# A vision block with attention scan and sixteen experts: low parts of three weight pieces moved from TensorE to VectorE, one row array per group, engine lists written anew

## The chip, the cores and the metric

The kernel runs on one core of one Trainium2 chip. The metric is the device time in microseconds (us) of one execution, where less is better. Each time below is one run, and the median of three is what counts. The profiled execution is a run of its own, with its own time.

## The reference

32 images of 96x96 are cut into 36 patches of 256 pixels each, projected to 192 channels, and a class token is put ahead, so each image has 37 rows. A block with a two-sided exponential scan over the rows (attention without a softmax matrix) and a gated square-ReLU layer is added, and then a mixture of 16 experts, of which each row takes 4 out of the 2 best of 4 groups, with 2 shared experts.

```python
h = concatenate([cls_tok, patches(x) @ W.T], axis=1)          # 32 x 37 x 192
# h = h + attention block(layernorm(h)):
x = layernorm(h); k, v, r = x @ Wk.T, x @ Wv.T, x @ Wr.T
y = bi_wkv(decay / T, first / T, k, v)                        # scans from both sides
x = x + sigmoid(r) * y @ Wo.T
g = ln(x); x = x + sigmoid(g @ Wr_f.T) * (square(relu(g @ Wk_f.T)) @ Wv_f.T)
# h = h + expert layer(layernorm(h)):
c = routing weights of 16 experts (sigmoid scores, top 2 of 4 groups, top 4, normalized, x 2.5)
hid = silu(x @ gWg + gbg) * (x @ gWu + gbu)                   # for each expert
out = sum(c * (hid @ gWd + gbd)) + shared experts
```

All is float32. A product with float32 accuracy is made of products of a rounded high part and the remaining low part of both factors.

## The kernel before, in words

The 1184 rows (32 images of 37) are worked on in four groups of 6, 10, 10 and 6 images: 222, 370, 370 and 222 rows. For each group there are these tracks of work, and the order lists name their steps as TRACK+GROUP:step.

- F, the front: patches to rows (tok0, tok1), normalization (stats1 to ln1), transposes and split into high and low part (tr1), products k, kt, v, rt, r, the two scans on VectorE (scan0, scan1, ab00 to ab11), exponentials on ScalarE (exps, weights), the quotient (recip, z), the output product (o0, o1) and the sum (x10, x1s, x1). Z:x0 on ScalarE makes the normalized rows that the sum starts from.
- M, the middle: normalization 2 (stats2 to ln2, tr2), the gate (rf), six pairs of an up product and a down product (up0 to up5, mix0 to mix5) with ReLU and square on ScalarE between them, the gated sum (gated, h1), normalization 3 (stats3 to ln3, tr3) and the routing (logits to routed).
- G, Y, S, X, D: the experts. 14 units (2 shared, 12 of 128 expert channels): TensorE makes a gate product (g0 to g13) and a value product (v1 to v13) into two PSUM banks, ScalarE applies SiLU (Y:e0 to e13), VectorE multiplies (S:s0 to s13) and applies the routing weights (X:x2 to x13), and TensorE adds up the outputs (D:d0 to d13). D:cT and C:cT transpose the routing weights and copy them; SyncE writes them to memory and spreads them over the partitions into the array gates.
- W, the weights: pieces of weights are loaded into a ring of four raw buffers. ScalarE copies each into its rounded high part (hi). The low part (lo) is raw - hi. For most pieces VectorE subtracts. For the six pieces of the experts, egu0 to egu5 (128 partitions, 1024 columns), the track L does it: TensorE multiplies raw by the identity and hi by the negative identity into PSUM array PA (L1162, L1163), and ScalarE copies PA into lo (L394). PA is also what the D steps add up into.

No engine chooses its next step at run time. PE_ORDER, ACT_ORDER, DVE_ORDER and POOL_ORDER are lists written out in the file; advance() runs the generator of each track up to the named step. Within a list each engine works strictly in order, and semaphores make it wait for what other engines owe it: a step that is not ready holds up all that stand behind it. SyncE's transfers stand in the order of the code. The ring buffer of a piece comes free when its low part is done.

Steps that need a neighbour: the experts of group g start at G:g0, once M:tr3 has split the normalized rows (stack3). ScalarE copies the rows of F:tok into the array h0, two of which serve four groups in turn; base holds the residual sum and h1 the rows after the middle, also two each. ScalarE's functions stand in tables: when the next activation needs another table than the last, an ACT_TABLE_LOAD stands ahead of it.

## Time and profile before

| | us |
|---|---|
| runs | 268.15, 268.33, 270.0 |
| median | 268.33 |
| profiled execution | 268.65 |
| its span | 266.8 |
| TensorE (PE) busy | 233.7 (88%) |
| VectorE (DVE) busy | 195.0 (73%) |
| ScalarE (ACT) busy | 147.6 (55%) |
| GpSimd (POOL) busy | 18.0 (7%) |

The span is the time from the first to the last instruction in the trace; the execution's own time lies 1.85 us above it. PE is TensorE's matmuls and PEld its weight loads, which overlap them; matmul ends are modelled, so neighbouring matmuls seem to overlap a little. The granted clock of TensorE is given as a share of 2.4 GHz. Times "from" and "at" are from the start of the span. A line number is that of the kernel before.

### The profile page before, as it was taken

Reading aid. Unit: us, or ns where it says so; the run is one execution under the profiler, and the core shown is the slowest. Engines: PE = TensorE matmul, PEld = TensorE weight load, DVE = VectorE, ACT = ScalarE, POOL = GpSimd, SP = SyncE. Lnnn points to the kernel's source line nnn. Section 1 sums busy time; section 2 is a strip of 40 time slices with the busy share of each in tenths; the row PEclk is TensorE's granted clock in tenths of the full one; section 3 lists DMA queues with packets and bytes.
Section 4 is the critical chain, followed back from the end, with each engine's and each line's share of the span. In section 5 each row is a group of like instructions: output and inputs, shape, how many; then the busy total and the mean of one; then the engine's idle time right before and its main releaser. Section 6 shows DMA issues by size and latency. Waiting matters only on the chain.

```text
span 266.8 us, 4316 instructions
## 1 busy us (share of the span) xinstructions
PE 233.7 (88%) x1436; PEld 211.5 (79%) x1436; DVE 195.0 (73%) x496; ACT 147.6 (55%) x305; POOL 18.0 (7%) x24
## 2 busy tenths in 40 slices
PE   0484968588878999999999999999999999999994
PEld 0373428465557899998999999999999999899993
DVE  4459898999997999989986599877731445654442
ACT  2489886989449997462756894144444332122220
POOL 4100402030011000030010000101000010000000
PEclk9998699999999999999999999999999999999999
DMA  5679550000000280000002430000014510014311
GB/s 150 210 254 337 176 184 2 0 0 0 0 2 1 47 195 2 2 0 0 4 26 68 174 105 4 0 1 0 2 30 160 164 37 2 1 35 106 68 34 37
DMA packets 12823, 17.49 MB, mean 66 GB/s; under 512 B 2144, under 2 KB 10882, under 8 KB 12674
## 3 DMA queue, kind: packets, MB, share of 16 engines
q1 hardware_dynamic: 11272, 16.20, 20.7%
q10 hardware_dynamic: 1530, 1.02, 1.4%
q8 instruction: 12, 0.20, 0.3%
q14 instruction: 9, 0.07, 0.1%
HBM read 16.22 MB, written 0.99 MB: 65 GB/s over the span
## 4 chain that ended last, share of the span: by engine, by line
PE 65%; DVE 16%; ACT 9%; issue 5%; DMA 2%; POOL 1%; SPq 0%; DVEq 0%; POOLq 0%; ACTq 0%
PE PG L958 17%; PE PA L978 15%; PE PG L960 11%; PE PF L978 4%; PE PA L1162 3%; DVE S L721 3%; PE PQ L958 2%; PE PX L995 2%; PE PF L995 2%; DVE K L745 2%; DMA w_tok<-in_w_tok 2%; PE PF L985 1%; DVE S L726 1%; DVE hid L901 1%; POOL rstd L374 1%
## 5 line engine op out<-in xcount | busy, mean ns | idle before, releaser
L553 ACT ACTIVATE act<-PG,columns 128x222 f32<-128x222 f32 (+3 forms) x56 | 28.4, 506 | 63.7 <-PE PG L960 60.0
L958 PE MATMUL PG<-stack,hi_egu 128*128 128x222 f32 (+1 forms) x288 | 62.1, 324 | 0.8 <-DVE hid L901 0.5
L901 DVE SCALAR_TENSOR_TENSOR hid<-PG,columns,act 128x222 f32<-128x222 f32 (+1 forms) x52 | 27.1, 520 | 30.9 <-PE PG L960 15.7
L958 PEld LDWEIGHTS PG<-stack,hi_egu 128*128 128x128 f32 x288 | 45.2, 190 | 4.9 <-DVE hid L901 2.9
L978 PE MATMUL PA<-w_ed,hid 128*124 128x192 f32 (+1 forms) x240 | 46.0, 327 | 0.7 <-DVE hid L914 0.7
L960 PE MATMUL PG<-stack,lo_egu 128*128 128x222 f32 (+1 forms) x192 | 42.7, 304 | 0.0
L978 PEld LDWEIGHTS PA<-w_ed,hid 128*124 128x124 f32 (+1 forms) x240 | 38.6, 183 | 1.1 <-issue 1.0
L960 PEld LDWEIGHTS PG<-stack,lo_egu 128*128 128x128 f32 x192 | 31.7, 190 | 0.0
L374 POOL TENSOR_TENSOR rstd<-var,minus_half 112x2 f32<-112x2 f32 (+3 forms) x12 | 15.2, 1266 | 198.7 <-DVE var L647 198.7
L914 DVE TENSOR_TENSOR hid<-hid,gates 128x222 f32<-128x222 f32 (+1 forms) x48 | 21.7, 463 | 8.2 <-DMA gates<-c_rows 7.4
L978 PE MATMUL PF<-w_down,mix_hid 128*124 128x192 f32 (+1 forms) x120 | 23.2, 327 | 0.2 <-ACT mix_hid L525 0.2
L978 PEld LDWEIGHTS PF<-w_down,mix_hid 128*124 128x124 f32 (+1 forms) x120 | 19.2, 183 | 0.5 <-ACT mix_hid L525 0.5
L1162 PE MATMUL PA<-gates,columns 128*128 128x512 f32 x24 | 14.4, 686 | 5.4 <-ACT hi_egu L383 3.3
L958 PE MATMUL PQ<-stack,hi_up 128*128 128x222 f32 (+1 forms) x72 | 15.9, 329 | 1.0 <-ACT relu L519 1.0
L519 ACT ACTIVATE relu<-PQ 128x222 f32<-128x222 f32 (+1 forms) x24 | 10.0, 415 | 12.1 <-PE PQ L960 12.1
L721 DVE TENSOR_TENSOR_SCAN S<-E,S 128x333 f32<-128x333 f32 (+1 forms) x16 | 16.3, 1066 | 0.0
L402 ACT ACTIVATE norm<-h,shift,rstd 124x192 f32<-124x192 f32 (+1 forms) x20 | 9.6, 537 | 7.1 <-DVE shift L653 7.1
L958 PEld LDWEIGHTS PQ<-stack,hi_up 128*128 128x128 f32 x72 | 11.3, 190 | 2.6 <-issue 2.6
L745 DVE RECIPROCAL K<-K 128x222 f32<-128x222 f32 (+3 forms) x8 | 11.9, 1520 | 0.1
L1162 PEld LDWEIGHTS PA<-gates,columns 128*128 128x128 f32 x24 | 4.6, 211 | 8.6 <-issue 8.3
L525 ACT ACTIVATE mix_hid<-relu 128x222 f32<-128x222 f32 (+1 forms) x24 | 10.8, 452 | 0.8
L667 DVE TENSOR_TENSOR stack<-full,stack 128x222 fp32r<-128x222 f32 (+3 forms) x16 | 7.4, 461 | 5.1 <-ACT full L413 4.9
(230 smaller groups left out, 418.6 us busy)
## 6 DMA issues: line engine op xcount, KB each, us to landing
gates<-in_w_egu SPq DMA_DIRECT2D x6, 512.0 KB, 4.0
gates<-c_rows SPq DMA_DIRECT2D x16, 138.8 KB, 2.8
gates<-c_rows SPq DMA_DIRECT2D x16, 92.5 KB, 2.7
w_ed<-in_w_ed SPq DMA_DIRECT2D x1, 1152.0 KB, 8.0
gates<-c_rows SPq DMA_DIRECT2D x12, 83.2 KB, 2.8
gates<-in_w_up SPq DMA_DIRECT2D x2, 384.0 KB, 3.7
pat<-in_patches SPq DMA_DIRECT2D x2, 370.0 KB, 4.2
gates<-c_rows SPq DMA_DIRECT2D x16, 46.2 KB, 2.6
```

The costliest lines, as they stand in the source:

```text
L374: nc.gpsimd.tensor_tensor(small[n]["rstd"][0:G.tp, 0:cols, 0:G.tiles], small[n]["var"][0:G.tp, 0:cols, 0:G.tiles], minus_half[0:G.tp, 0:co ...
L525: nc.scalar.activation(mix_hid[:, m % 2, 0:G.n], relu[:, 0:G.n], ACT.Square).then_inc(act_square, 1)
L553: nc.scalar.activation(act[128 - gate:128, n % 2, 0:G.n], PG[0:gate, gate_bank(n), 0:G.n], ACT.Silu, bias=bias).then_inc(act_silu, 1)
L721: step(V_.tensor_tensor_scan(run(x, d), run(E1[:, d * WK:d * WK + wk], d), run(x, d), 0.0, ALU.mult, ALU.add))
L745: step(V_.reciprocal(K[:, s], K[:, s]))
L901: V_.scalar_tensor_tensor(out, PG[part, 1, 0:G.n], bias, act[part, i, 0:G.n], ALU.add, ALU.mult).then_inc(mul_done, 1)
L914: V_.tensor_tensor(out, out, gates[:, n - SCH, 0:G.n], ALU.mult).then_inc(hid_ready, 1)
L958: mm(out, w_hi[:, slot, cols], x[:, p, 0:G.n], start=(p == 0), stop=False, skip_group_check=True)
L960: last = mm(out, w_lo[:, p, cols], x[:, p, 0:G.n], start=False, stop=(p == 1), skip_group_check=True)
L978: last = mm(tile_out(P, G, t), src[:, G.ts[t]:G.ts[t] + G.tp], w, start=start and t != 1, stop=stop, skip_group_check=True)
L995: last = mm(out, src[:, G.ts[t]:G.ts[t] + G.tp], w, start=(i == 0 and t == a), stop=(i == len(parts) - 1), skip_group_check=True)
L1162: mm(PA[:, k, 0:512], ident32, raw[n % RING][:, 512 * k:512 * k + 512], start=True, stop=False, skip_group_check=True)
```

## The change

It does five things.

1. The low parts of egu0, egu1 and egu2 stay with TensorE and ScalarE; those of egu3, egu4 and egu5 are made by VectorE with one subtraction each, as for the other pieces.
2. Each group has an array of its own for its rows (stream), which holds in turn what h0, base and h1 held. The waits that guarded the reuse of those arrays go away. Some other arrays are shared: norm2 is x1, norm3 is gate_r, Zm is the front of V, and ReLU writes into mix_hid, where the square is taken in place. The waits that these need are added or moved.
3. The array gates gets HELD = 4 periods of 3 chunks, of which there are 4, by way of gate_slot.
4. SyncE fetches group 3's patches ahead of group 0's gate rows.
5. The lists of TensorE, ScalarE and VectorE are written anew. POOL_ORDER stays.

```diff
 PERIODS = ECH // 3
+HELD = 4
-LOW_ON_PE = [p[0] for p in PIECES if p[0].startswith("egu")]
+LOW_ON_PE = [p[0] for p in PIECES if p[0] in ("egu0", "egu1", "egu2")]
+LOW_ON_DVE = [p[0] for p in PIECES if p[0] not in LOW_ON_PE]
...
-        gates = sb("gates", [128, ECH, N])
-        flat_gates = gates[:, :, :].rearrange("p c n -> p (c n)")
-        raw = [flat_gates[:, i * RING_COLS:(i + 1) * RING_COLS] for i in range(RING)]
+        gates_raw = sb("gates", [128, max(3 * HELD * N, RING * RING_COLS)])
+        gates = gates_raw[:, 0:3 * HELD * N].rearrange("p (c n) -> p c n", n=N)
+        raw = [gates_raw[:, i * RING_COLS:(i + 1) * RING_COLS] for i in range(RING)]
+
+        def gate_slot(g, chunk):
+            return (g * ECH + chunk) % (3 * HELD)
...
-        h0 = [sb(f"h0_{i}", [TP, TILES, C]) for i in range(2)]
+        stream = [sb(f"h_{g}", [G.tp, G.tiles, C]) for g, G in enumerate(GROUP)]
         x1, gate_r = (sb(n, [TP, TILES, C]) for n in ("x1", "gate_r"))
-        base, h1 = ([sb(f"{n}_{i}", [TP, TILES, C]) for i in range(2)] for n in ("base", "h1"))
-
-        norm = [None, *(sb(f"norm{i}", [TP, TILES, C]) for i in (1, 2, 3))]
+
+        norm = [None, sb("norm1", [TP, TILES, C]), x1, gate_r]
         full = [None, *(sb(f"full{i}", [128, 2, N]) for i in (1, 2))]
...
-        Zm = sb("Zm", [128, N])
+        Zm = V[:, 0:N]
...
-        relu, mix_hid = sb("relu", [128, N]), sb("mix_hid", [128, 2, N])
+        mix_hid = sb("mix_hid", [128, 2, N])
...
                 if g == 0:
                     sp.wait_ge(lo_done, len(PIECES) - len(LOW_ON_PE))
                     sp.wait_ge(pe_low, len(LOW_ON_PE))
-                    for first, periods, done in ((0, 1, gates_in[0]), (1, PERIODS - 1, gates_in[1])):
+                    for first, periods, done in ((0, 1, gates_in[0]), (1, HELD - 1, gates_in[1])):
...
-                    return
                 for j in range(PERIODS):
-                    if g:
-                        sp.wait_ge(hid_ready, at(hid_ready, g - 1, 3 * (j + 1)))
+                    q = g * PERIODS + j - HELD
+                    if q < 0:
+                        continue
+                    sp.wait_ge(hid_ready, at(hid_ready, q // PERIODS, 3 * (q % PERIODS + 1)))
...
-                        sp.dma_start(gates[a:b, 3 * j + chunk, 0:n],
+                        sp.dma_start(gates[a:b, gate_slot(g, 3 * j + chunk), 0:n],
...
             for n in range(13, len(PIECES)):
                 piece(n)
             patches(2)
+            patches(3)
             gates_across(0)
-            patches(3)
             for g in range(1, len(GROUP)):
                 gates_across(g)
             for g in range(len(GROUP)):
...
             G, P = GROUP[g], front_banks(g)
             for bank, a, b in G.banks:
                 act_e.wait_ge(pe_tok, at(pe_tok, g, bank + 1))
-                if g >= 2 and bank == 0:
-                    act_e.wait_ge(x1_ready, at(x1_ready, g - 2, 1))
-                nc.scalar.activation(h0[g % 2][0:G.tp, a:b, :], rows_of(P[bank], G, a, b), ACT.Copy).then_inc(tok_out, 3 - G.rounds)
+                nc.scalar.activation(stream[g][0:G.tp, a:b, :], rows_of(P[bank], G, a, b), ACT.Copy).then_inc(tok_out, 3 - G.rounds)
                 yield f"tok{bank}"
             act_e.wait_ge(rstd_ready[1], at(rstd_ready[1], g, 1))
...
             act_e.wait_ge(pe_kvr, at(pe_kvr, g, 2))
             tails(K, lower, lower)
             yield "kt"
+            since(act_e, pe_o, g)
             tails(V, upper, upper)
             yield "vt"
             act_e.wait_ge(act_kvr, at(act_kvr, g, 2))
...
         def act_first_rows(act_e, g):
             G = GROUP[g]
-            since(act_e, norm_ready[2], g)
+            since(act_e, pe_transposed[2], g)
...
                     since(act_e, act_square, g)
                 else:
                     act_e.wait_ge(act_square, at(act_square, g, m))
-                nc.scalar.activation(relu[:, 0:G.n], PQ[:, 0:G.n], ACT.Relu).then_inc(act_relu, 1)
-                act_e.wait_ge(act_relu, at(act_relu, g, m + 1))
                 if m >= 2:
                     act_e.wait_ge(pe_mix, at(pe_mix, g, m - 1))
                 elif m == 0:
                     since(act_e, pe_mix, g)
-                nc.scalar.activation(mix_hid[:, m % 2, 0:G.n], relu[:, 0:G.n], ACT.Square).then_inc(act_square, 1)
+                nc.scalar.activation(mix_hid[:, m % 2, 0:G.n], PQ[:, 0:G.n], ACT.Relu).then_inc(act_relu, 1)
+                act_e.wait_ge(act_relu, at(act_relu, g, m + 1))
+                nc.scalar.activation(mix_hid[:, m % 2, 0:G.n], mix_hid[:, m % 2, 0:G.n], ACT.Square).then_inc(act_square, 1)
                 yield f"mix{m}"
             act_e.wait_ge(rstd_ready[3], at(rstd_ready[3], g, 1))
-            act_norm_rows(act_e, g, 3, h1[g % 2])
+            act_norm_rows(act_e, g, 3, stream[g])
...
             yield "x1s"
             v.wait_ge(x1_out, at(x1_out, g, 2))
             rs = (slice(0, G.tp), slice(0, G.tiles))
-            V_.tensor_tensor(base[g % 2][rs], h0[g % 2][rs], x1[rs], ALU.add).then_inc(x1_ready, 1)
+            V_.tensor_tensor(stream[g][rs], stream[g][rs], x1[rs], ALU.add).then_inc(x1_ready, 1)
             yield "x1"
         def edge_e1(wk):
...
             v.wait_ge(act_rf, at(act_rf, g, 1))
             v.wait_ge(pe_mix, at(pe_mix, g, UPS))
-            if g >= 2:
-                v.wait_ge(out_stored[g - 2], 16 * GROUP[g - 2].tiles)
-            h = h1[g % 2]
+            x = stream[g]
             for bank, a, b in G.banks:
                 step(V_.scalar_tensor_tensor(gate_r[0:tp, a:b, :], gate_r[0:tp, a:b, :], 1.0, rows(PF, G, bank, a, b), ALU.add, ALU.mult))
             yield "gated"
             settle()
-            step(V_.scalar_tensor_tensor(h[rs], gate_r[rs], 0.5, base[g % 2][rs], ALU.mult, ALU.add))
+            step(V_.scalar_tensor_tensor(x[rs], gate_r[rs], 0.5, x[rs], ALU.mult, ALU.add))
             yield "h1"
             settle()
...
 PE_ORDER = _order(
-    "F0:tok0 F0:tr1a F0:tr1b F1:tok0 F0:k F0:kt F1:tok1 F0:v F0:rt F0:r L:egu0 F1:tr1a F1:tr1b L:egu1 L:egu2 F0:o0 F1:k",
+    "F0:tok0 F0:tr1a F0:tr1b F1:tok0 F0:k F1:tok1 F0:kt F0:v F0:rt F0:r L:egu0 F1:tr1a F1:tr1b L:egu1 F0:o0 F1:k F1:kt F1:v",
...
-    "M0:mix2 M0:up4 M0:mix3 M0:up5 M0:mix4 M0:mix5 F2:tr1b L:egu5 F1:o0 F1:o1 M0:tr3 F2:k M0:logits G0:g0 F2:kt G0:g1 G0:v1",
-    "F2:v G0:g2 F2:rt D0:cT G0:v2 G0:g3 D0:d1 D0:d0 M1:tr2 G0:v3 F2:r G0:g4 G0:v4 G0:g5 M1:rf M1:up0 D0:d2 D0:d3 G0:v5 D0:d4",
-    "G0:g6 G0:v6 F3:tok0 D0:d5 G0:g7 G0:v7 D0:d6 G0:g8 M1:up1 G0:v8 M1:mix0 M1:up2 G0:g9 D0:d7 M1:mix1 M1:up3 G0:v9 G0:g10",
+    "M1:tr2 F2:r G0:v2 G0:g3 F3:tok0 G0:v3 G0:g4 D0:cT D0:d1 D0:d0 M1:rf M1:up0 G0:v4 G0:g5 M1:up1 M1:mix0 M1:up2 M1:mix1",
...
 ACT_ORDER = _order(
-    "F2:exps F2:weights Y0:e6 F3:tok0 Y0:e7 M1:rf M1:mix0 Y0:e8 M1:mix1 Y0:e9 M1:mix2 M1:mix3 M1:mix4 Y0:e10 F3:ln1 M1:mix5",
+    "M0:logits Y0:e0 Y0:e1 F2:kf F2:v M1:ln2 Y0:e2 F2:rt M1:tr2 Y0:e3 F2:r F2:exps C0:cT Z2:x0 Y0:e4 M1:rf M1:mix0 Y0:e5",
+    "F3:tok0 M1:mix1 M1:mix2 F2:weights M1:mix3 Y0:e6 F3:ln1 Y0:e7 M1:mix4 Y0:e8 F3:tr1a F3:tr1b M1:mix5 Y0:e9 Y0:e10 Y0:e11",
...
 DVE_ORDER = _order(
+    "W:egu3 F0:x1s F0:x1 M0:stats2 M0:mean2 F1:scan0 M0:var2 F1:scan1 M0:ln2 F1:e1 F1:sb0 W:egu4 F1:sb F1:top0 F2:stats1",
+    "M0:var3 F2:tr1 F1:x1s M0:ln3 F1:x1 W:egu5 M0:tr3 M1:stats2 M0:biased M1:mean2 M0:logits M1:var2 F2:scan0 S0:s0",
...
```

The lists move steps in many places. Three of them follow, as the built programs have them; instructions of a kind that follow each other stand in one row with their count.

VectorE, from the statistics of group 0's third normalization (M0:mean3) to the subtractions of M0:tr3 (stack_0), before:

```order
L647 TENSOR_SCALAR var<-mv 112x2
L759 TENSOR_TENSOR x<-x,PX 124x384
L653 SCALAR_TENSOR_TENSOR shift<-mv,rstd 112x2
L667 TENSOR_TENSOR stack<-full,stack 128x370
L667 TENSOR_TENSOR stack<-full,stack 64x370
L759 TENSOR_TENSOR x<-x,PX 124x192
L765 TENSOR_TENSOR base<-h_1,x 124x576
L667 TENSOR_TENSOR stack_0<-PF,stack_0 128x222
L667 TENSOR_TENSOR stack_0<-PF,stack_0 64x222
```

The same place now:

```order
L763 TENSOR_TENSOR x<-x,PX 124x384
L651 TENSOR_SCALAR var<-mv 112x2
L671 TENSOR_TENSOR stack<-full,stack 128x370
L671 TENSOR_TENSOR stack<-full,stack 64x370
L763 TENSOR_TENSOR x<-x,PX 124x192
L657 SCALAR_TENSOR_TENSOR shift<-mv,rstd 112x2
L769 TENSOR_TENSOR h<-h,x 124x576
L602 TENSOR_TENSOR lo_egu<-gates,hi_egu 128x1024
L671 TENSOR_TENSOR stack_0<-PF,stack_0 128x222
L671 TENSOR_TENSOR stack_0<-PF,stack_0 64x222
```

The low part of egu5 stands directly ahead of M0:tr3, and the shift of ln3 has moved behind F2:tr1 and F1:x1s.

TensorE, from group 0's last down products of the middle (L978, M0:mix) to the transposes of M0:tr3 (PF from norm), before:

```order
L958 MATMUL PQ<-stack,hi_up 128x222 x3
L960 MATMUL PQ<-stack,lo_up 128x222 x2
L978 MATMUL PF<-w_down,mix_hid 112x192 x4
L985 MATMUL PX<-columns,norm 128x124 x3
L1162 MATMUL PA<-gates,columns 128x512
L1163 MATMUL PA<-hi_egu,minus_ident 128x512
L1162 MATMUL PA<-gates,columns 128x512
L1163 MATMUL PA<-hi_egu,minus_ident 128x512
L995 MATMUL PX<-w_o,Zm 124x192 x2
L995 MATMUL PX<-w_o,Zt 124x192 x2
L995 MATMUL PX<-w_o,Zm 124x192
L995 MATMUL PX<-w_o,Zt 124x192
```

The same place now, up to M0:tr3 and F2:kt:

```order
L960 MATMUL PQ<-stack,hi_up 128x222 x3
L962 MATMUL PQ<-stack,lo_up 128x222 x2
L980 MATMUL PF<-w_down,mix_hid 112x192 x4
L997 MATMUL PX<-w_o,V 124x192 x2
L997 MATMUL PX<-w_o,Zt 124x192 x2
L997 MATMUL PX<-w_o,V 124x192
L997 MATMUL PX<-w_o,Zt 124x192
L960 MATMUL PX<-stack,hi_k 128x370 x3
L962 MATMUL PX<-stack,lo_k 128x370 x2
L987 MATMUL PF<-columns,gate_r 128x112 x4
L960 MATMUL PX<-stack,hi_k 128x370 x3
L962 MATMUL PX<-stack,lo_k 128x370 x2
```

Nothing stands between the last down products and the o products of group 1 (PX from w_o) any more, and both k products of group 2 stand ahead of the router's products.

ScalarE, around the exponentials of group 2 (E, S and mx in place; R is the last), before:

```order
L553 ACTIVATE act<-PG,columns 128x222
L472 ACT_TABLE_LOAD
L472 ACTIVATE E<-E,columns 128x2x370
L472 ACTIVATE E<-E,columns 128x2x185
L473 ACTIVATE S<-S 128x2x555
L477 ACTIVATE mx<-mx 128x555 x2
L480 ACTIVATE mx<-mx 128x555
L481 ACTIVATE R<-R 128x555
L553 ACT_TABLE_LOAD
L553 ACTIVATE act<-PG,columns 128x222
```

Now the first half of it:

```order
L476 ACT_TABLE_LOAD
L476 ACTIVATE E<-E,columns 128x2x370
L476 ACTIVATE E<-E,columns 128x2x185
L477 ACTIVATE S<-S 128x2x555
L568 ACTIVATE hid_s<-PQ 17x222
L493 ACTIVATE x<-h,shift,rstd 124x192 x3
L557 ACT_TABLE_LOAD
L557 ACTIVATE act<-PG,columns 128x222
```

And, eleven rows later, the second:

```order
L481 ACT_TABLE_LOAD
L481 ACTIVATE mx<-mx 128x555 x2
L484 ACTIVATE mx<-mx 128x555
L485 ACTIVATE R<-R 128x555
L527 ACTIVATE mix_hid<-PQ 128x370
L529 ACTIVATE mix_hid<-mix_hid 128x370
L557 ACT_TABLE_LOAD
L557 ACTIVATE act<-PG,columns 128x222
```

The program before has six table loads, the changed one eight.

## Rows read from the trace of the kernel before

**Rows 1.** The page: busy us per engine, and busy tenths in 40 slices.

```profile
PE 233.7 (88%) x1436; PEld 211.5 (79%) x1436; DVE 195.0 (73%) x496; ACT 147.6 (55%) x305; POOL 18.0 (7%) x24
...
PE   0484968588878999999999999999999999999994
...
DVE  4459898999997999989986599877731445654442
```

**Rows 2.** Busy time in four stretches: us of each engine, clock, DMA.

```profile
20.00:80.00 60.00, 44.00 (x210) 30.72 (x209) 56.20 (x108) 46.23 (x94) 7.39 (x4) 0.94 0.23 78
80.00:104.00 24.00, 22.31 (x153) 20.28 (x153) 21.36 (x63) 21.71 (x41) 0.85 (x1) 1.00 0.31 68
104.00:224.00 120.00, 119.47 (x773) 115.75 (x773) 87.53 (x239) 60.46 (x132) 5.95 (x6) 1.00 0.14 43
224.00:267.00 43.00, 38.56 (x270) 36.77 (x268) 20.52 (x64) 8.88 (x19) 0.00 (x0) 1.00 0.19 44
```

**Rows 3.** VectorE in order of time: start, us, instruction, idle before.

```profile
29.72 0.17 DVE L653 SCALAR_TENSOR_TENSOR shift<-mv,rstd 124x6 f32<-124x6 f32 x1 [1.22 <-POOL rstd L374]
...
55.45 1.32 DVE L715 TENSOR_TENSOR S<-S,V 128x1110 f32<-128x1110 f32 x1
...
78.41 0.80 DVE L667 TENSOR_TENSOR stack<-PF,stack 128x222 fp32r<-128x222 f32 x2
```

**Rows 4.** TensorE in order of time.

```profile
26.97 2.05 PE L1162 MATMUL PA<-gates,columns 128*128 128x512 f32 x2 [3.32 <-ACT hi_egu L383]
...
69.14 0.90 PE L978 MATMUL PF<-w_down,mix_hid 128*112 128x192 f32 x4 [0.21 <-ACT mix_hid L525]
...
70.20 1.03 PE L1162 MATMUL PA<-gates,columns 128*128 128x512 f32 x2
...
73.68 0.89 PE L995 MATMUL PX<-w_o,Zm 128*124 128x192 f32 x4 [1.13 <-issue]
...
75.93 0.59 PE L995 MATMUL PX<-w_o,Zm 128*124 128x192 f32 x2 [0.71 <-DVE x L759]
...
80.51 0.68 PE L958 MATMUL PX<-stack,hi_k 128*128 128x370 f32 x3
81.03 0.50 PE L960 MATMUL PX<-stack,lo_k 128*128 128x370 f32 x2
81.37 0.49 PE L958 MATMUL PG<-stack,hi_sgu 128*128 128x222 f32 x3
```

**Rows 5.** Line 598: operation, count, shortest/median/longest ns, starts.

```profile
L598 DVE TENSOR_TENSOR lo_r<-gates,hi_r x1: 685/685/685, 13.2 to 13.2; 128x512 fp32r<-128x512 f32 x1
...
L598 DVE TENSOR_TENSOR lo_sgu<-gates,hi_sgu x1: 951/951/951, 25.4 to 25.4; 128x768 fp32r<-128x768 f32 x1
```

**Rows 6.** VectorE's waits from 0 to 80: total us, times, longest.

```profile
DVE shift L653 <- POOL rstd L374: 2.7, 3, 1.2
...
DVE x L759 <- PE PF L995: 0.6, 1, 0.6
...
DVE stats L635 <- ACT x L489: 0.4, 1, 0.4
```

**Rows 7.** GpSimd in order of time.

```profile
26.99 2.69 POOL L374 TENSOR_TENSOR rstd<-var,minus_half 124x6 f32<-124x6 f32 x1 [14.22 <-DVE var L647]
```

**Rows 8.** ScalarE in order of time, ahead of 80 us.

```profile
52.92 1.41 ACT L472 ACTIVATE E<-E,columns 128x740 f32<-128x740 f32 x2
54.23 1.11 ACT L473 ACTIVATE S<-S 128x1110 f32<-128x1110 f32 x1
...
62.07 1.05 ACT L383 ACTIVATE hi_egu<-gates 128x1024 fp32r<-128x1024 f32 x1
```

**Rows 9.** ScalarE in order of time, behind 80 us.

```profile
94.93 1.28 ACT L472 ACT_TABLE_LOAD   x1
```

**Rows 10.** Busy time in two stretches; the clock is the number before the last two.

```profile
25.00:31.00 6.00, 4.03 (x6) 1.84 (x6) 4.78 (x13) 5.34 (x11) 2.69 (x1) 0.50 0.76 271
32.00:38.00 6.00, 4.43 (x15) 2.11 (x14) 5.83 (x9) 5.42 (x8) 0.00 (x0) 1.00 0.53 160
```

32 lines of the change are left out of this document (16 added, 16 removed), and 97 rows, old and new, of tables (ACT_ORDER, DVE_ORDER, PE_ORDER).

## The prediction

> **What bounds the kernel now.** I read the engines' busy times and the forty slices first, then the busy times of four stretches, then VectorE's waits, then the instructions in order of time around the places where the lists differ. By the shares TensorE is the busiest (233.7 us of 266.8), but its slices show two different kernels: in its first thirteen slices, until 87 us, the digits are mostly 4 to 8, and from there on all are 9 but the last; VectorE's row is the other way round, 8s and 9s with one 7 from 20 to 133 us, and 7s and less over the last third [rows 1]. In numbers: from 20 to 80 us VectorE is busy for 56.2 of 60 us and TensorE for 44.0; from 80 to 104 us TensorE has 22.3 of 24; from 104 to 224 us it has 119.5 of 120 [rows 2]. So there is a first part, which ends when group 0's rows are normalized for the experts (M0:tr3, the two subtractions at 78.41 us [rows 3]) and which VectorE sets, and a second part, which TensorE sets. A microsecond of TensorE is worth something only if it is removed behind that point; a microsecond of VectorE is worth something only ahead of it, or where TensorE waits for it.
>
> **The low parts.** Three pieces leave TensorE. The last of them began at 70.20 us and was over 1.13 us, the idle time that stands in the next row, before 73.68 us: some 2.3 us, so 6.9 us leave TensorE, and three copies from PSUM leave ScalarE. All three stood in the first part, and behind the last one TensorE sat idle because VectorE's z of group 1 was not there yet [rows 4]. Cover is what is removed here, not path: I cost the removal itself at 0. It becomes idle time of TensorE unless something else is pulled ahead.
>
> VectorE gets three subtractions over 1024 columns. The trace has none of that width; the nearest are 951 ns for 768 columns and 685 ns for 512 [rows 5], 266 ns per 256 columns, so 1.22 us, and 1.18 us from start to start since neighbours overlap a little: **+3.5 us** for three. All three stand ahead of M0:tr3, the last directly ahead of it (first order listing), and no other VectorE work crosses that point, so the whole 3.5 us fall into the part that VectorE sets.
>
> **What the new lists give back on VectorE.** Until 80 us VectorE's waits hold three that the lists fill: 1.2 us of the 2.7 us for GpSimd's root, the one before the shift at 29.72 us [rows 3, 6], 0.6 us for group 0's o product, and 0.4 us ahead of group 2's statistics [rows 6]. Group 1's variance now goes out ahead of F0:e1, some 4 us of VectorE work before the shift that needs it, where the root took 2.69 us [rows 7]; W:egu3 stands where the 0.6 us wait was, W:egu4 ahead of the 0.4 us one. **-2.2 us**.
>
> **What they cost on ScalarE.** Group 1's F1:sa started at 55.45 us [rows 3], right when ScalarE's exponentials (52.92 us, then 54.23 us for 1.11 us) ended: there both engines are tight. The copy hi_egu5, 1.05 us, stood at 62.07 us and now stands ahead of these exponentials [rows 8]. I leave 0.3 us of it to ScalarE's short idle times, so **+0.75 us**; the ends are 0 and 1.05 us.
>
> First part together: 3.5 - 2.2 + 0.75 = +2.0 us until the experts of group 0 can start.
>
> **Second part.** TensorE's own list for it is shorter by one step: F2:kt, at 80.51 us behind the start of G0, is now done ahead of it: 0.86 us from its start at 80.51 us to the next product at 81.37 us [rows 4]. **-0.85 us**. From 80 to 104 us TensorE was idle for 24 - 22.3 = 1.7 us [rows 2]. F3:tok0 can fill some of that: group 3's patches are now fetched before group 0's gate rows, and the product stands between G0:g3 and G0:v3 instead of behind G0:v6. F2:scan0 also stands in VectorE's wait for the first SiLU. I take **-1.0 us**; the ends are 0 and -1.7 us. Behind 104 us there is no idle to win [rows 2], and the lists of group 3's experts, which make the tail, are the same in both kernels.
>
> **ScalarE's table loads.** The third pair of listings shows what the names of the steps hide. F2:exps and F2:weights stood together between two SiLU; now SiLU steps stand between them, so the function table is changed twice more in this stretch. A change takes 1.28 us [rows 9], so 2.57 us more for an engine that has 21.7 of 24 us busy there [rows 2]. Who waits: behind the second new load stands e6, and G0:g7 waits for e6. Between G0:g5 and G0:g7 TensorE's new list puts M1:up1 to up4, mix0 to mix2 and three D0 steps: up1 to up4 alone make 3.4 us by the 0.86 us of F2:k, which has the same five products over 370 columns [rows 4], more than both loads. I take 0; the ends are 0 and +2.6 us.
>
> **Edits at no cost.** One array per group: the sum into stream takes the place of the sum into base, one VectorE instruction for another; the wait for the stores of group g-2 falls away at M2 and M3, where TensorE is full whatever VectorE does [rows 2]. The gate array holds four periods, as many as there are, so slots and waits of its transfers stay. ReLU and square still are two ScalarE instructions; the wait for mix(m-2), now ahead of ReLU, is met, since TensorE issues mix(m-2) ahead of up(m). Zm in V: F1:vt must wait for F0:o, which stands ahead of F1:k. x0 now waits for TensorE's transposes M0:tr2 instead of for the norm: that is in the 0.75 us.
>
> **Sum.** +2.0 - 0.85 - 1.0 + 0 = +0.15 us on a profiled execution of 268.65 us: 268.8 us. That execution lies 0.3 us above the median of the runs, 268.33 us, so **268.5 us**. What a measurement of this kernel can tell from no change is about 1%, 2.7 us: faster means below 265.65, slower above 271.0.
>
> **Rivals.** *TensorE's saving comes through* (25%). VectorE's 3.8 us of idle time between 20 and 80 us [rows 2] would take in 3.3 us of the added 3.5, the exponentials would not be late, and TensorE would fill all its 1.7 us: +3.5 - 3.3 - 0.85 - 1.7 = -2.35 us, and up to -3.5 us if VectorE's idle time from 80 to 104 us (24 - 21.4 us [rows 2]) closes by another 1.2 us: 265.9 to 264.8 us, 265.3 us in the middle. For it: TensorE is the busiest engine and loses 6.9 us [rows 1, 4]. Against it: none of the 6.9 us lay in the part that TensorE sets.
>
> *ScalarE's table loads uncover* (18%). One place: e4 to e6 of group 0. If M1's steps are not ready when the list wants them, TensorE stands before G0:g5 or G0:g7 for both loads. +2.6 us on the sum: 271.1 us, **slower**. It decides from the point where e6 comes later than TensorE has work between g5 and g7; every microsecond behind that is TensorE's. For it: with 21.7 of 24 us busy ScalarE has 2.3 us to spare [rows 2], less than 2.6 us. Against it: M1's steps are early in all lists.
>
> *TensorE's clock falls* (15%). In the trace TensorE idled for 3.32 us before 26.97 us [rows 4], and from 25 to 31 us its granted clock was 0.50, 1.2 instead of 2.4 GHz; from 32 to 38 us it was 1.00 [rows 10]. The mean from 20 to 80 us is 0.94 [rows 2], which the fall at 25 us makes up alone, so the gap of 1.13 us before 73.68 us [rows 4] brought none. With the piece at 70.20 us gone, TensorE has nothing between M0:mix5, which started at 69.14 us [rows 4], and F1:o0, which waits for z at about 73.7 us: a gap of some 4 us, longer than the one that went with the fall. At half clock F1:o0 (two products of 0.89 us), F1:o1 (two of 0.59 us) and F2:k (0.86 us) take 3.8 us more [rows 4], and all stand ahead of M0:tr3, which leads to the experts. About half of it lies beside VectorE's work of the same time, so +1.9 us on the sum, 270.4 us. The Trainium skill, page "TensorE: Matmul & The Clock Gate", section "Why this matters for your kernels", warns of just this: longer idle gaps between bursts of matmuls take the engine back to half rate. By that rule the lower clock comes for certain, and the sum would be 270.4 us; the trace agrees with it at 26.97 us, and has no such gap at this place.
>
> The forecast itself has 42%. That the change would not do what it says is excluded: the built program has three pieces on each engine.
>
> **From the cases.** Faster by over 1%: two thirds of the first rival (17%) and the lower end of the forecast (5%), 22%. Slower by over 1%: half of the second (9%), a third of the third (5%) and the upper end of the forecast (4%), 18%. Within 1%: 60%. The range goes from the first rival's middle less 0.4 us, 264.9 us, to just above the second rival's time, 271.2 us; the forecast's own is 266.8 to 270.2 us.
>
> **What would show it.** VectorE's M0:tr3 at 80.4 us instead of 78.4; its three new rows at 1.2 us each; no wait of over 0.5 us for the root before F1:ln1; F1:sa at 56.2 us; TensorE's stretch behind 104 us as full as before; eight table loads instead of six; and the granted clock between 70 and 80 us, 1.00 if I am right in my sum. I would be wrong in the sum if M0:tr3 stood at 79 us or earlier, and wrong in the mechanism if TensorE showed idle time behind 104 us.

## The result, and the profile after

In its first set of runs the changed kernel took 271.35 us in the median (268.79 to 273.04, 20 runs) against 268.5 us (267.84 to 270.7, 20 runs) for the kernel before in the same set: a ratio of 1.006, 95% interval 1.004 to 1.009. In a second set it took 269.89 us (12 runs) against 269.44 us (23 runs), ratio 1.0025 [0.998, 1.007]. Ratios leave out runs more than 1.5% above the fastest of their kernel; medians are of all runs. So it is slower by 0.6% in the first set, and by 0.3% in the second, whose interval takes in no change. Both are within the 1% that the forecast called no change. The forecast of 268.5 us lay 1.4 to 2.9 us below the two medians, and the first of them lies 0.15 us above the end of the forecast's range, 271.2 us; taken as a ratio to the 268.33 us that the forecast started from, it is 269.9 us. The profiled execution took 270.15 us, 1.50 us more than before's 268.65 us. In both kernels the runs fall into groups of spans up to 4 us apart, of which more stands at the end; the median of a set depends on how many fall into each, so spans are compared by their shortest group.

The page of the changed kernel, to be held against [rows 1], and its busy time in four stretches (us of PE, PEld, DVE, ACT and POOL, granted clock, DMA share, GB/s), against [rows 2]:

```profile
PE 229.7 (86%) x1418; PEld 211.7 (79%) x1418; DVE 197.5 (74%) x499; ACT 147.2 (55%) x304; POOL 19.3 (7%) x24
...
PE   0484678479678799999999999999999999999992
...
DVE  4469999999998999899787299986821365844442
```

```profile
20.00:80.00 60.00, 41.38 (x190) 31.39 (x191) 57.98 (x106) 44.05 (x91) 6.78 (x4) 0.83 0.25 88
80.00:104.00 24.00, 21.43 (x147) 19.55 (x147) 22.68 (x69) 22.13 (x45) 1.78 (x1) 1.00 0.14 33
104.00:224.00 120.00, 119.60 (x781) 116.24 (x779) 85.03 (x233) 60.92 (x128) 6.97 (x6) 1.00 0.15 46
```

The two parts are still there: VectorE 58.0 of 60 us ahead of 80 us, TensorE 119.6 of 120 behind 104 us. VectorE in order of time, against [rows 3]:

```profile
26.41 0.16 DVE L657 SCALAR_TENSOR_TENSOR shift<-mv,rstd 124x6 f32<-124x6 f32 x1
...
40.48 1.23 DVE L602 TENSOR_TENSOR lo_egu<-gates,hi_egu 128x1024 fp32r<-128x1024 f32 x1
...
49.23 1.22 DVE L602 TENSOR_TENSOR lo_egu<-gates,hi_egu 128x1024 fp32r<-128x1024 f32 x1
...
55.67 1.31 DVE L719 TENSOR_TENSOR S<-S,V 128x1110 f32<-128x1110 f32 x1
...
76.17 1.11 DVE L671 TENSOR_TENSOR stack<-full,stack 128x370 fp32r<-128x370 f32 x2
77.31 0.35 DVE L763 TENSOR_TENSOR x<-x,PX 124x192 f32<-124x192 f32 x1
77.58 0.15 DVE L657 SCALAR_TENSOR_TENSOR shift<-mv,rstd 112x2 f32<-112x2 f32 x1
...
78.38 1.22 DVE L602 TENSOR_TENSOR lo_egu<-gates,hi_egu 128x1024 fp32r<-128x1024 f32 x1
79.76 0.81 DVE L671 TENSOR_TENSOR stack<-PF,stack 128x222 fp32r<-128x222 f32 x2 [0.16 <-ACT stack L421]
```

The new rows take 1.22 us, the wait for GpSimd's root ahead of the first is gone, and M0:tr3 stands at 79.76 us, 1.35 us later than before.

The end is what I had left out. The last additions and the stores behind them, in order of time, of the kernel before and then of the changed one:

```profile
255.54 1.16 ACTq L572 DMA_DIRECT2D out<-h  x3
...
263.36 0.56 DVE L920 TENSOR_TENSOR h<-h,PA 112x384 f32<-112x384 f32 x1 [1.06 <-PE PA L978]
263.95 0.87 ACTq L572 DMA_DIRECT2D out<-h  x2
```

```profile
259.99 3.88 ACTq L576 DMA_DIRECT2D out<-h  x5
...
262.54 0.55 DVE L922 TENSOR_TENSOR h<-h,PA 112x384 f32<-112x384 f32 x1 [1.06 <-PE PA L980]
```

The row of five in the second fence starts with group 2's three stores (O2:out) and ends with group 3's two (O3:out); between them ScalarE waits for the last addition, so its 3.88 us are not the time that the issues take. The last addition ends at 263.92 us before and at 263.09 us after: **the computation is 0.83 us shorter**. Yet the whole is 1.5 us longer. I split each profiled execution at three points: M0:tr3, the end of the last addition, and the end of the span.

| us | before | after | difference |
|---|---|---|---|
| start to M0:tr3 | 78.41 | 79.76 | +1.35 |
| M0:tr3 to the last addition | 185.51 | 183.33 | -2.18 |
| last addition to the span's end | 2.88 | 4.21 | +1.33 |
| the execution's time above its span | 1.85 | 2.85 | +1.00 |
| sum | 268.65 | 270.15 | +1.50 |

The last two stores are issued within 0.9 us of the last addition in both kernels. What differs is how much of the stores' data is still to be moved then. Queue q10 carries it; its packets from the end of the last addition to the end of the span, before (263.92 to 266.8 us) and after (263.09 to 267.3 us):

```profile
q10 hardware_dynamic: 249, 0.17, 21.0%
```

```profile
q10 hardware_dynamic: 469, 0.33, 27.2%
```

Group 3's two stores have 249 packets; in after 220 packets of group 2's three stores are still behind the last addition. In before all of those were done by then.

Behind the span's end the trace of after has one packet of code on queue q8. This is all that moves in the window from 266.8 to 271 us:

```profile
DMA packets 1, 0.02 MB, mean 4 GB/s; under 512 B 0, under 2 KB 0, under 8 KB 0
## 3 DMA queue, kind: packets, MB, share of 16 engines
q8 instruction: 1, 0.02, 1.9%
```

In before the last packet on q8 starts 3.5 us ahead of the span's end.

### The profile page after: what moved, and what is told of

Read it like the earlier page. It is cut to its first block and busy times, and to the rows that moved or that the text cites. A ratio compares the mean times of both kernels' runs of the same rounds, so it can differ in the third digit from the quotient of the medians.

```text
span 267.3 us, 4259 instructions
## 1 busy us (share of the span) xinstructions
PE 229.7 (86%) x1418; PEld 211.7 (79%) x1418; DVE 197.5 (74%) x499; ACT 147.2 (55%) x304; POOL 19.3 (7%) x24
## 5 line engine op out<-in xcount | busy, mean ns | idle before, releaser
L379 POOL TENSOR_TENSOR rstd<-var,minus_half 112x2 f32<-112x2 f32 (+3 forms) x12 | 16.5, 1379 | 198.9 <-DVE var L651 198.9
L980 PE MATMUL PF<-w_down,mix_hid 128*124 128x192 f32 (+1 forms) x120 | 23.9, 334 | 0.7 <-ACT mix_hid L529 0.7
L980 PEld LDWEIGHTS PF<-w_down,mix_hid 128*124 128x124 f32 (+1 forms) x120 | 19.8, 187 | 1.2 <-ACT mix_hid L529 1.0
L960 PE MATMUL PQ<-stack,hi_up 128*128 128x222 f32 (+1 forms) x72 | 17.1, 349 | 2.2 <-ACT mix_hid L527 2.2
L527 ACT ACTIVATE mix_hid<-PQ 128x222 f32<-128x222 f32 (+1 forms) x24 | 10.0, 415 | 11.7 <-PE PQ L962 11.6
L960 PEld LDWEIGHTS PQ<-stack,hi_up 128*128 128x128 f32 x72 | 12.4, 208 | 3.5 <-issue 3.5
L1164 PE MATMUL PA<-gates,columns 128*128 128x512 f32 x12 | 8.5, 793 | 5.0 <-ACT hi_egu L388 5.0
L962 PE MATMUL PQ<-stack,lo_up 128*128 128x222 f32 (+1 forms) x48 | 11.4, 321 | 0.0
L529 ACT ACTIVATE mix_hid<-mix_hid 128x222 f32<-128x222 f32 (+1 forms) x24 | 10.8, 451 | 0.8
L407 ACT ACTIVATE gate_r<-h,shift,rstd 124x192 f32<-124x192 f32 (+1 forms) x10 | 4.8, 538 | 9.9 <-DVE shift L657 9.9
```

The lines of the kernel that those rows point to most:

```text
L379: nc.gpsimd.tensor_tensor(small[n]["rstd"][0:G.tp, 0:cols, 0:G.tiles], small[n]["var"][0:G.tp, 0:cols, 0:G.tiles], minus_half[0:G.tp, 0:co ...
L527: nc.scalar.activation(mix_hid[:, m % 2, 0:G.n], PQ[:, 0:G.n], ACT.Relu).then_inc(act_relu, 1)
L529: nc.scalar.activation(mix_hid[:, m % 2, 0:G.n], mix_hid[:, m % 2, 0:G.n], ACT.Square).then_inc(act_square, 1)
L960: mm(out, w_hi[:, slot, cols], x[:, p, 0:G.n], start=(p == 0), stop=False, skip_group_check=True)
L962: last = mm(out, w_lo[:, p, cols], x[:, p, 0:G.n], start=False, stop=(p == 1), skip_group_check=True)
L980: last = mm(tile_out(P, G, t), src[:, G.ts[t]:G.ts[t] + G.tp], w, start=start and t % 2 == 0, stop=stop, skip_group_check=True)
```

## The experiments

I held three theories on where the 1.5 us come from. A, the clock: without the products that filled its gaps TensorE falls to half clock once more. B, VectorE: its three subtractions make the experts start later. C: the two table loads more on ScalarE. D to G came with what the runs showed. All kernels ran in sets of five rounds beside the kernel before. The table gives each profiled execution by the four parts above, the spans of the shortest group of the set's runs, and the ratio as defined above. Seven of e_tail_tables' twelve runs are not in its ratio: their spans are 271.1 to 271.8 us, and the median of all twelve is 273.92 us.

| run | to M0:tr3 | to last addition | to span's end | above span | shortest group | ratio [95%] |
|---|---|---|---|---|---|---|
| after2 | 79.81 | 183.34 | 4.15 | 2.58 | 266.8-267.3 | 1.0025 [0.998, 1.007] |
| e_split | 81.78 | 186.48 | 2.74 | 1.87 | 269.4-269.8 | 1.012 [1.006, 1.017] |
| e_lists | 87.51 | 183.36 | 4.13 | 1.82 | 271.6 | 1.021 [1.016, 1.027] |
| e_warm | 79.94 | 183.30 | 4.16 | 2.39 | 266.7-267.4 | 1.0045 [1.000, 1.009] |
| e_tail | 79.39 | 183.40 | 2.71 | 2.77 | 265.3-265.7 | 1.000 [0.997, 1.004] |
| e_late | 80.55 | 185.43 | 4.12 | 1.90 | 267.2-268.2 | 1.005 [1.002, 1.008] |
| e_tail_pool | 88.78 | 184.12 | 2.70 | 2.65 | 272.1-272.4 | 1.023 [1.018, 1.028] |
| e_tail_tables | 81.88 | 187.13 | 2.79 | 2.85 | 267.6-268.1 | 1.004 [1.000, 1.008] |
| e_tail_double | 82.93 | 183.37 | 2.70 | 2.58 | 268.9-269.3 | 1.014 [1.008, 1.019] |
| e_tail_warm0 | 81.16 | 183.59 | 2.75 | 1.90 | 265.1-265.9 | 0.997 [0.993, 1.001] |
| e_tail_pad | 79.78 | 183.35 | 2.77 | 1.77 | 265.5-266.2 | 0.997 [0.993, 1.001] |
| e_best | 81.90 | 183.93 | 2.77 | 1.78 | 265.9-266.5 | 0.999 [0.996, 1.003] |

The traces of e_lists, e_late, e_tail_pool, e_tail_tables and e_best belong to longer groups, in which TensorE gets fast late (last section), so their first column stands some 2 us high. Those of e_split (span 271.0 us) and e_tail_warm0 (267.5 us) are also of longer runs, but without that late start.

**The changed kernel again.** 

> The changed kernel once more, as the reference of this set. Theory A (clock): its time depends on how much of the stretch 20 to 80 us TensorE spends at the lower of its two levels (granted clock 0.50 in the rows), so runs fall into groups: spans near 267 us with a mean clock near 0.96 and spans near 269 us with 0.935; a trace of the second kind would show one more stretch at 0.50 that costs about 2 us before the fourteenth expert's start is reached. Theory B (VectorE): the time above before is the 1.36 us by which the first expert starts later, in every run, and the rest is scatter. Theory C (ScalarE's table loads): the six to eight loads of 1.28 us each behind 80 us take 2.6 us from TensorE's feeding between 80 and 104 us. All: ratio to before about 1.006.

Its spans show the two groups that A speaks of (seven at 266.8 to 267.3 us, three at 269.1 to 269.3 us) and two runs above them, at 270.4 and 270.9 us. Its trace is of the first group and like after's.

**The move of the three pieces alone**, on the lists of before:

```diff
-LOW_ON_PE = [p[0] for p in PIECES if p[0].startswith("egu")]
+LOW_ON_PE = [p[0] for p in PIECES if p[0] in ("egu0", "egu1", "egu2")]
```

L:egu3 to L:egu5 leave TensorE's and ScalarE's lists; on VectorE W:egu3 stands ahead of F0:x1s, W:egu4 behind F1:sb0, W:egu5 ahead of M0:tr3. ScalarE's copy of egu5's high part moves forward, to behind F1:v.

> Only the move of three low parts: the lists, the buffers and the rest of before are kept, the second half of the pieces (3, 4, 5) is subtracted by VectorE at the places that the change gives them, and TensorE's and ScalarE's steps for them are left out. Theory A (clock): TensorE's gaps in 45 to 75 us are no longer filled, the granted clock falls to 0.50 a second time there; time as after or worse, 270.5 to 273 us. Theory B (VectorE): three subtractions of 1.2 us without what the new lists give back: the first expert starts up to 3.5 us later than in before, 271 to 272 us, with the granted clock as in before. Theory C (table loads): six loads as in before, so no loss, 268.3 us.

M0:tr3 comes 3.37 us later than in before, theory B's number, and the shortest span is 3.5 us longer (269.4 against 265.9 us). But the number is made up otherwise than B has it. F1:sa starts 1.37 us later (56.82 against 55.45 us) behind two subtractions, the third adds 1.1 us, and 0.87 us come between them, where no subtraction stands. VectorE waits there for TensorE's last down products of the middle:

```profile
74.18 0.55 DVE L793 SCALAR_TENSOR_TENSOR gate_r<-gate_r,PF 112x384 f32<-112x384 f32 x1 [0.72 <-PE PF L979]
```

Four such products took 1.48 us at 69.78 us, 0.81 us in before (at 68.11 us). So the clock has a share in M0:tr3, and in the part behind it, which is 0.97 us longer. Busy time of e_split in three stretches; the clock is the number before the last two:

```profile
60.00:70.00 10.00, 7.73 (x36) 7.43 (x36) 9.86 (x11) 4.76 (x11) 0.60 (x1) 0.67 0.00 0
70.00:80.00 10.00, 7.26 (x36) 6.09 (x35) 8.77 (x19) 3.68 (x8) 0.69 (x1) 0.87 0.00 0
80.00:90.00 10.00, 8.55 (x40) 8.18 (x39) 8.03 (x41) 5.69 (x13) 0.85 (x1) 0.66 0.01 2
```

The granted clock is below 1.00 in 80 to 90 us, where TensorE begins to set the time. In before it is 1.00 throughout 80 to 104 us [rows 2]. So theory A's second fall of the clock and B's later start are both in this run. It can't part them by its time, which is within A's range and, with a median of 272.79 us, 0.8 us above B's.

**The lists alone**, all six pieces with TensorE and ScalarE:

```diff
-LOW_ON_PE = [p[0] for p in PIECES if p[0] in ("egu0", "egu1", "egu2")]
+LOW_ON_PE = [p[0] for p in PIECES if p[0].startswith("egu")]
```

On TensorE L:egu2 stands ahead of M0:tr2, L:egu3 behind M0:rf, L:egu4 behind M0:up2, L:egu5 behind M0:mix5, on ScalarE accordingly.

> Only the new lists and buffers: all six low parts stay with TensorE and ScalarE, and VectorE makes none of them. Theory A (clock): the added products fill TensorE's gaps before 75 us, so the clock does not fall a second time; with the lists' gain on VectorE about 266 to 268 us. Theory B (VectorE): the three subtractions of 1.2 us are gone from VectorE, so the first expert starts 1.4 to 3.5 us earlier than in after, 267 to 269 us, whatever the clock does. Theory C (table loads): the eight loads are still there, so about as slow as after, 270 to 271.5 us. A and B are told apart by the granted clock in 45 to 65 us.

None of the three: its shortest span is 271.6 us, 4.8 us longer than after2's. The places are mine, not the change's, and they are bad ones: the piece ahead of M0:tr2 makes VectorE wait 2.57 us for ScalarE at 56.05 us. It shows that these pieces are not free on TensorE wherever they stand, but not what the new lists are worth; the column to the last addition does (below).

**Products in TensorE's gaps**, in after:

```diff
+                for k in range(2):
+                    for _ in range(5):
+                        mm(PA[:, k, 0:512], minus_ident[:, :], hi["egu0"][:, k, :], start=True, stop=True, ...)
...
-... M0:tr2 F2:tok1 M0:rf ...
+... M0:tr2 F2:tok1 H0:w0 M0:rf ...
...
-... M0:mix4 M0:mix5 F1:o0 ...
+... M0:mix4 M0:mix5 H0:w1 F1:o0 ...
```

> After, with 20 products of 512 columns more on TensorE (two groups of ten, into a bank that is free there; nothing reads their results): one group ahead of the first FFN's relu step, where TensorE stands idle for 3.6 us at 50 to 53.7 us, one ahead of the second group's output step, where it stands idle for up to 2 us at 72 us. VectorE's and ScalarE's lists are those of after. Theory A (clock): the granted clock stays at 1.00 behind 35 us or falls once less, the runs no longer fall into two groups, spans 266.5 to 267.5 us, time about 269.5 us (ratio to before 1.000 to 1.004). Theory B (VectorE): the first expert's start is set by VectorE and doesn't move; time as after, 271.3 us, ratio 1.006. Theory C: as B.

Busy time from 52 to 62 us, of after and of e_warm:

```profile
52.00:62.00 10.00, 6.93 (x30) 6.66 (x31) 9.94 (x19) 8.60 (x17) 2.30 (x1) 0.51 0.05 19
```

```profile
52.00:62.00 10.00, 6.12 (x34) 5.07 (x33) 9.94 (x19) 8.70 (x17) 2.31 (x1) 0.86 0.05 18
```

The clock comes back, VectorE does the same 9.94 us, M0:tr3 (79.94 us) and the end stay where they were, and the runs still fall into groups (seven of twelve in the shortest, as in after2). Theory A falls for after: the additional half clock is real and lies beside VectorE's work.

**The end of the list**, in after (e_tail) and, the other way, in before (e_late):

```diff
-... Y3:e9 Y3:e10 Y3:e11 Y3:e12 Y3:e13 O2:out O3:out
+... Y3:e9 Y3:e10 O2:out Y3:e11 Y3:e12 Y3:e13 O3:out
```

> After, with one entry of ScalarE's list moved: the stores of group 2's rows are issued ahead of expert step 11 of group 3, as in before, not behind step 13. In the traces of after the last addition on VectorE ends at 263.09 us, 0.83 us earlier than in before (263.96), yet the span is 0.5 us longer: five store issues of 3.9 us stand together at the end of ScalarE's queue, where before has two. Theory D (the end of the list): the whole loss is there; from the last addition to the end of the span it takes 4.2 us in after and 2.9 us in before, and outside the span 2.6 to 2.8 us against 1.85. Moved back, the span is 266.0 us and the time 267.8 us (266.9 to 268.3), 2.1 us less than after, faster than before by 0.2 to 0.4%. Theory B (VectorE's three subtractions set the start of the experts): the stores lay beside each other anyway, no change against after, ratio to before 1.003 to 1.006.

> Before, with that one entry moved the other way: the stores of group 2's rows behind expert step 13, all else as in before. Theory D (the end of the list): last addition as in before (263.9 us), the way from there to the end 2.1 us longer, 270.4 us or a ratio of 1.008. Theory B: ratio 1.000.

Both are right in part. The way from the last addition to the span's end goes from 4.15 to 2.71 us in the one and from 2.88 to 4.12 us in the other, the shortest spans by -1.5 and +1.3 us. The packets of q10 behind the last addition follow: 249 in e_tail, 469 in e_late, as in before and after. It is this data that takes the time, not the 3.9 us of store issues that the expectation speaks of: the last issue is over 0.8 us behind the last addition in e_tail and 1.1 us in e_late. e_tail's median, 270.16 us, misses the 267.8 us expected, since only five of its twelve runs fell into the shortest group. The time above the span doesn't follow: it stays at 2.0 to 2.9 us in the one and at 1.82 to 1.92 us in all twelve runs of the other. So it has another cause.

**The three pieces on GpSimd**, from e_tail:

```diff
...
+                pool.wait_ge(hi_done, n + 1)
+                nc.gpsimd.tensor_tensor(lo[name][:, :, :], src, hi[name][:, :, :].bitcast(F32), ALU.subtract).then_inc(pool_low, 1)
...
```

> The kernel of the run e_tail, with the low parts of pieces 3 to 5 subtracted by GpSimd (behind its reciprocal root of the second norm of group 0, at 45 us, where it then stands idle until 57 us) and not by VectorE. Theory B (VectorE's subtractions delay the first expert): VectorE is 3.5 us less busy ahead of the router's transposition at 79.76 us, it comes 1 to 3 us earlier, and so does the end: 265 to 267 us. Rival 1 (the delay is not VectorE's): as e_tail, 267.8 us. Rival 2 (GpSimd and VectorE slow each other down, or GpSimd takes over 4 us for one subtraction, so that the root of the first norm of group 2 behind them at 57 us comes late): later than e_tail, 268.5 to 271 us.

The second rival, and worse than I put it. GpSimd, then VectorE, of this run in order of time:

```profile
48.28 6.94 POOL L390 TENSOR_TENSOR lo_egu<-gates,hi_egu 128x1024 fp32r<-128x1024 f32 x3
...
48.35 6.90 DVE L669 SCALAR_TENSOR_TENSOR shift<-mv,rstd 112x2 f32<-112x2 f32 x1 [0.53 <-POOL rstd L382]
```

An instruction over two columns that takes 0.16 us elsewhere lasts 6.90 us, as long as GpSimd's three: VectorE stands still. The Trainium skill, page "SBUF — State Buffer", section "SBUF: two separate sides", says that the two engines share a pair of ports under an exclusive lock held for the whole instruction. The trace agrees, and shows it held over three instructions in a row.

**Two table loads fewer**, from e_tail:

```diff
-... C0:cT Z2:x0 Y0:e4 M1:rf M1:mix0 Y0:e5 F3:tok0 M1:mix1 M1:mix2 F2:weights M1:mix3 ...
+... C0:cT Z2:x0 F2:weights Y0:e4 M1:rf M1:mix0 Y0:e5 F3:tok0 M1:mix1 M1:mix2 M1:mix3 ...
```

> The kernel of the run e_tail, with group 2's weight exponentials on ScalarE ahead of expert step 4, right behind its first exponentials, which takes away the second change of the table (six loads in place of eight, 2.6 us less on ScalarE). Theory C (the loads cost time by keeping TensorE short of activated rows between 80 and 104 us): TensorE's busy time in that window rises from 21.4 us, the end comes 0.5 to 2.6 us earlier, 265.2 to 267.3 us. Rival (the loads are covered by VectorE and TensorE; what e4 waits for comes 3.5 us later instead): no change or up to 1.5 us slower, 267.8 to 269.3 us.

The part behind M0:tr3 grows by 3.7 us in its trace, the shortest span of its set by 2.3 us. The move takes two loads away and delays a SiLU step at once, so by its time alone it doesn't tell what the loads cost. The traces do. TensorE's waits from 80 to 112 us, all of after's and the two longest of this run (total us, times, longest):

```profile
PE PX L997 <- ACT R L470: 1.2, 1, 1.2
PE PG L960 <- DVE hid_s L903: 1.1, 1, 1.1
PE PF L987 <- ACT x L407: 0.2, 1, 0.2
```

```profile
PE PG L960 <- ACT act L557: 1.5, 1, 1.5
PE PX L997 <- ACT R L470: 1.2, 1, 1.2
```

In after TensorE never waits for a SiLU step (act) there, although two more loads stand ahead of such steps; the wait of 1.2 us for R is over at 91.33 us, ahead of both. Theory C falls: the loads are covered. Here TensorE waits 1.5 us for the step that I put behind the exponentials; what makes up the rest of the 3.7 us I have not traced.

**The three subtractions made twice**, from e_tail:

```diff
+                        V_.tensor_tensor(lo[name][:, :, :], src, hi[name][:, :, :].bitcast(F32), ALU.subtract).then_inc(once, 1)
+                        v.wait_ge(once, ...)
```

> The kernel of the run e_tail, with each of the three subtractions on VectorE made twice (the second waits for the first), so VectorE is 3.7 us busier at the places where the change put them. Theory B (VectorE sets the experts' start, and its time reaches the end): the router's transposition of group 0 moves from 79.4 us to 83 us, and the shortest span of the set from 265.3 us to 268.5 to 269.0 us. Rival (the filling of TensorE between 80 and 104 us takes much of a later start back): 266 to 267.5 us. In both the time from the last addition to the end stays at 2.7 us.

M0:tr3 is 3.54 us later, the part behind it the same to 0.03 us, the shortest span 3.6 us longer: **time added to VectorE ahead of M0:tr3 reaches the end one for one.**

**Products ahead of the first transposes**, from e_tail:

```diff
+                for _ in range(12):
+                    mm(PA[:, 0, 0:C], whole["tok"][:, 0, 0:128], whole["tok"][:, 1, :], start=True, stop=True, ...)
...
-    "F0:tok0 F0:tr1a ...
+    "F0:tok0 H0:w0 F0:tr1a ...
```

> The kernel of the run e_tail, with 12 products of 192 columns more on TensorE (nothing reads them) in the 4.5 us for which it stands idle at 9.6 to 14.1 us. Theory E (an early clock): what parts the runs of every kernel here into spans 2 us apart is whether TensorE's products reach full speed at about 17.5 us or only behind 22 us; in the second kind group 0's key products take 0.98 us instead of 0.59 us and group 1's third row tile reaches ScalarE 1.5 us later. With work ahead the products are at full speed from 14.1 us on in all runs: group 1's eight row products take 1.4 us instead of 2.8 us, all spans lie within 0.6 us of each other, at or below the shortest of e_tail (265.3 us), time 266.5 to 268.3 us. Rival (the parting comes from elsewhere, or the added work only uses up the allowance and the clock falls to half a little later): spans still 2 to 3 us apart, median as e_tail's (270 us) or later.

Half right. Group 1's eight row products are at full speed (1.48 us) in its trace and the longest span is 267.7 us in place of 269.0 us, but the runs still fall into two groups (five at 265.1 to 265.9 us, seven at 266.8 to 267.7 us), and the median, 268.75 us, lies outside the 266.5 to 268.3 us expected. The trace is of the second group, its M0:tr3 at 81.16 us in spite of the early speed; its granted clock is 0.85 from 40 to 50 us, where e_tail's is 1.00. Whether that parts the runs of this kernel I have not shown. My added products also ran to 15.0 us, past the 14.1 us at which the transposes could have started.

**More instructions for TensorE**, from e_tail:

```diff
+                for _ in range(times):
+                    mm(PA[0:32, 0, 0:32], minus_ident[:, 0:32], hi["egu0"][:, 0, 0:32], start=True, stop=True, ...)
```

> The kernel of the run e_tail, with 80 products of 32 columns more on TensorE (160 instructions; nothing reads them), 56 in its idle time at 50 us and 24 in that at 72 us, places where added work changed no time in the run e_warm. Theory F (a block of code fetched behind the end): in after and e_tail the device time is 2.4 to 2.9 us longer than the span, in before 1.85 us, and the traces show a packet of 16 KB on the code queue q8 1 to 2 us behind the span's end in the first two, where before has its last one 4 us ahead of it. With more instructions in TensorE's program its blocks shift, the last one comes ahead of the end, and the time is 1.85 us above the span again: 0.8 us less than e_tail at like spans. Rival (the longer way out comes from something else in the new lists): 2.4 to 2.9 us as in e_tail.

In all twelve runs the time lies 1.75 to 1.88 us above the span, in e_tail's twelve 1.96 to 2.88 us; the last two packets on q8 start 28 and 11 us ahead of the end, none behind it. Theory F holds: 160 instructions that compute nothing shorten the median time above the span from 2.68 to 1.82 us, at like spans. In e_tail_warm0 48 instructions more, at the head of the program, did the same (1.77 to 1.92 us in all twelve runs); in e_warm 40 more did not (2.39 to 2.87 us in eleven of twelve).

**The last subtraction later**, from e_tail_pad:

```diff
-    "M0:var3 F2:tr1 F1:x1s M0:ln3 F1:x1 W:egu5 M0:tr3 M1:stats2 M0:biased M1:mean2 M0:logits M1:var2 F2:scan0 S0:s0",
+    "M0:var3 F2:tr1 F1:x1s M0:ln3 F1:x1 M0:tr3 M1:stats2 M0:biased M1:mean2 M0:logits M1:var2 F2:scan0 S0:s0 W:egu5",
```

> The kernel of the run e_tail_pad, with the last of the three subtractions (piece 5, 1.22 us at 78.4 us) moved on VectorE from ahead of the router's transposition of group 0 to behind the gate of the first expert (about 83 us). Its result is first read by the thirteenth expert step, long after 100 us. Theory B, as the run e_tail_double has it (VectorE's time ahead of the experts reaches the end one for one): the transposition comes 1.2 us earlier (78.6 us), the shortest spans fall from 265.5 to 264.3 us, time about 266.4 us, faster than before by 0.8%. Rival G (VectorE is as full from 80 to 104 us as before it, 22.7 of 24 us, and TensorE waits for it there): the 1.2 us are only moved behind the start, spans 265.3 to 265.9 us as in e_tail_pad, and 267.6 us.

No gain: the shortest span is 0.4 us longer, rival G's case or a little worse. VectorE ahead of M0:tr3 in this run (a longer group):

```profile
79.72 0.15 DVE L657 SCALAR_TENSOR_TENSOR shift<-mv,rstd 112x2 f32<-112x2 f32 x1
79.84 0.76 DVE L769 TENSOR_TENSOR h<-h,x 124x576 f32<-124x576 f32 x1
81.90 0.81 DVE L671 TENSOR_TENSOR stack<-PF,stack 128x222 fp32r<-128x222 f32 x2 [1.30 <-ACT stack L421]
```

Where the subtraction had stood, VectorE now waits 1.30 us. M0:tr3 comes 2.18 us behind the shift, in after too (77.58 to 79.76 us): that is the way over ScalarE's normalization, TensorE's transposes and ScalarE's copy. So the third subtraction was free where the change put it.

## Why the prediction was right, and where it was not

- **The mechanism** was right for after: adding to VectorE ahead of M0:tr3 reaches the end (e_tail_double), 20 products put back on TensorE in the first part change nothing (e_warm), and TensorE sets the second part. "I cost the removal itself at 0" holds with the new lists only. With the old ones (e_split) TensorE's longer idle time brought the lower clock, and VectorE waited 0.72 us for it.
- **VectorE +3.5 us.** Right as a price for one subtraction after another: each takes 1.22 us, and three more cost 3.54 us in e_tail_double. That e_split's M0:tr3 is 3.37 us later is not this price: the subtractions account for 2.5 us of it. In after only two of the three are paid. Up to F1:x10 VectorE is 0.35 us later than before (75.67 against 75.32 us), with two subtractions of 1.22 us done: the lists gave back 2.1 us, my term was 2.2. The third lies in a wait, as e_best showed. What makes M0:tr3 late is a move that I had not priced: the last step of group 0's statistics, M0:var3, now stands behind F1:x10, and M0:ln3 behind F2:tr1 and F1:x1s. GpSimd's root between the two, before and after:

```profile
75.39 0.70 POOL L374 TENSOR_TENSOR rstd<-var,minus_half 112x2 f32<-112x2 f32 x1 [16.16 <-DVE var L647]
```

```profile
76.34 0.92 POOL L379 TENSOR_TENSOR rstd<-var,minus_half 112x2 f32<-112x2 f32 x1 [16.90 <-DVE var L651]
```

  The root is there at 77.26 instead of 76.09 us, and the shift of M0:ln3 comes at 77.58 instead of 76.11 us, 1.47 us later. Of this 1.17 us are there once the root is, 0.35 us of them VectorE's lateness up to F1:x10; M0:ln3's own place adds 0.3 us. The worth of either place alone was not run.
- **ScalarE +0.75 us.** The term was nothing: ScalarE's exponentials ended at 55.21 us, before at 55.34 us. F1:sa came at 55.67, not at 56.2 us, 0.2 us later than before, behind VectorE's own work. First part together: +1.35 us, forecast +2.0 us.
- **Second part -1.85 us** (F2:kt and TensorE's refill). Measured -2.18 us, and the same to 0.1 us in six further traces with these lists; in e_tail_warm0, e_best and e_tail_pool it is -1.4 to -1.9 us. The size is near by luck, since the -1.0 us for idle time filled did not come. TensorE is idle for 2.6 us from 80 to 104 us, not for less than 1.7, and the step that was to fill it makes a wait of its own, F3:tok0 for ScalarE's copy of R:

```profile
91.33 1.52 PE L997 MATMUL PX<-w_tok,pat 128*112 128x192 f32 x8 [1.16 <-ACT R L470]
```

  From the router's products to the last addition TensorE's busy time falls from 181.1 to 178.3 us while its idle time rises from 3.6 to 4.1 us. F2:kt, ahead of M0:logits now, accounts for 0.85 us of the busy time (the term of that size was right); where the other 1.9 us come from stays open.
- **Table loads 0.** Eight are there, and after's trace has no wait of TensorE behind the added ones.
- **The clock at 70 to 75 us** stayed at 1.00, as the sum had it, but the rival's case did not arise: the gap of some 4 us ahead of F1:o0 was 1.45 us, since M0:mix5 started at 71.38, not at 69.14 us. The clock fell at another place, from 52 to 62 us, beside VectorE's work, and the fall began in a gap of 3.56 us; before had 2.82 us there and no fall. The two gaps in after:

```profile
53.68 0.87 PE L970 MATMUL PF<-hi_rf,stack 128*112 128x192 f32 x3 [3.56 <-DVE stack L671]
...
73.73 0.89 PE L997 MATMUL PX<-w_o,V 128*124 128x192 f32 x4 [1.45 <-issue]
```

  The lower clock that the rival feared does reach the experts in e_split. The rule of the Trainium skill that the prediction cites (page "TensorE: Matmul & The Clock Gate", section "Why this matters for your kernels") agrees with the gap of 3.56 us in after, where it costs nothing. The fall in e_split that costs, from 80 to 90 us, came with no idle time longer than 1.52 us since 68 us, so the rule does not cover it.
- **What failed is a term that was not in the sum.** "... the lists of group 3's experts, which make the tail, are the same in both kernels" overlooked ScalarE's O2:out, which moved from ahead of Y3:e11 to behind Y3:e13: +1.33 us, with group 2's data still to be moved behind the last addition. The sum also took the 1.85 us above the span as given; it became 2.35 to 3.07 us in 14 of the first set's 20 runs and stayed at 1.78 to 1.94 us in six. Together +2.3 us, against errors of -0.65 and -0.33 us: 268.8 + 2.3 - 0.65 - 0.33 = 270.1 us, the profiled 270.15.

Neither correction makes a version that is faster beyond doubt. The best, e_tail_pad, has a median of 267.84 us against 269.41 us, ratio 0.997 [0.993, 1.001]. So the change comes out within the 1% because a shorter computation (-0.83 us) and a longer way out (+2.3 us) partly cancel, not because the forecast's terms were all right.

## What to carry to other kernels

Split a profiled execution at the points where the bound changes, down to the time above the span, and hold the parts against each other: here four parts of +1.35, -2.18, +1.33 and +1.00 us hid behind a result of half a per cent. When lists are written anew, read their last entries too, stores above all: an entry that cost nothing amid the work costs 1.3 us at the end, because its data is still being moved when the last results are ready. A subtraction that stands in a wait is free; ask for each moved step which chain it lengthens before counting its duration.

## What the runs showed of the hardware

**The moment at which TensorE gets fast differs from run to run, by over 4 us.** The same products (group 0's F0:k) in after and in e_best:

```profile
18.18 0.59 PE L960 MATMUL PF<-stack,hi_k 128*128 128x222 f32 x3
```

```profile
18.32 0.98 PE L960 MATMUL PF<-stack,hi_k 128*128 128x222 f32 x3
```

In the second kind products last 0.98 us until 22 us, and group 1's third row tile reaches VectorE's statistics after a wait of 1.77 instead of 0.28 us; M0:tr3 is 2.1 to 2.5 us later (81.88 in e_tail_tables, 79.76 us in after, 79.39 us in e_tail). The granted clock of both rows reads 1.00, so here the durations tell the speed and the clock column doesn't; in e_late and e_tail_tables it reads 0.50 for the same slow products from 20 us on. In both kinds TensorE had been idle for 4.47 us before 14.1 us. The Trainium skill, page "TensorE: Matmul & The Clock Gate", section "What's actually happening", says that the moment of the change of speed varies from run to run; the traces agree. The same section of the Trainium skill puts the variation at half a microsecond either way, which the traces do not bear out: fast by 18.2 us in after, not before 22 us in e_best. It also calls the price of the ramp under 1% of a typical kernel's time, which 2.1 of 267 us is, but that is more than the whole change was worth. That every longer group comes from this I have not shown; e_tail_warm0's does not.

**Code loading can lie behind the end.** A packet of 16 KB on q8 behind the span's end goes with 2.4 to 2.9 us above the span (seven traces), its absence with 1.8 to 1.9 us (seven, before's among them). The Trainium skill, page "Runtime: NRT & Kernel Launch", section "Instruction fetch mechanics", states that each engine's instructions are fetched in blocks of 16 KB while it executes, and that a branch to a block not loaded waits for it. The packet's size agrees; no run shows which instruction waited. That this queue serves TensorE's program follows only from e_tail_pad and e_tail_warm0, where instructions added to TensorE alone moved its packets. In some runs of e_lists, e_split and after the time above the span was near 2.9 us, in others of the same program 1.8 us, so the place of a block's border is not all.

**A store's data outlasts its issue.** The five store issues of after are over 0.78 us behind the last addition (263.87 us), but 469 packets of theirs are moved behind it, and the span ends at 267.3 us. In before 249 are, and it ends 2.88 us behind the last addition instead of 4.21 us.
